# A routed adapter kernel: one chunk of the first weight is asked for behind two copies of x

## The reference

```python
def reference(x, itok_B_3_7, L0_cond_weight):
    # x (128, 32, 512) f32, itok_B_3_7 (128,) int32 from 3 to 7, L0_cond_weight (8, 512, 512) f32
    w = L0_cond_weight[itok_B_3_7]
    return x + jnp.einsum('bsi,boi->bso', x, w)
```

## Time and profile before

| | |
|---|---|
| median of three runs | 108.26 us (107.31 to 108.94) |
| the profiled execution, its own time | 106.55 us |
| its span in the trace | 104.8 us |
| TensorE busy | 98.7 us, 94% of the span |
| VectorE, ScalarE, GpSimd busy | 53.0, 56.0 and 42.4 us |
| granted clock of TensorE, mean | 0.994 |
| moved by DMA | 22.92 MB, 219 GB/s on average |

### The profile page before, as it was taken

How to read it: one execution, slowest core, us unless ns; L and a number is a source line. 1 busy time by engine, 2 the same in 40 slices (tenths; PEclk the granted TensorE clock), 3 DMA queues, 4 the chain that set the end, 5 groups by cost and what they waited for, 6 DMA issues and landing times.

```text
span 104.8 us, 2302 instructions
## 1 busy us (share of the span) xinstructions
PE 98.7 (94%) x447; PEld 80.3 (77%) x447; DVE 53.0 (51%) x107; ACT 56.0 (53%) x103; POOL 42.4 (40%) x58
## 2 busy tenths in 40 slices
PE   5969999999999999999999999999999999999960
PEld 3538888888888888888888888888888888888830
DVE  1289972595206964690378424862458247701000
ACT  5048333496424972883379443964388439633220
POOL 6757135007530466066304860276114731743000
PEclk9999999999999999999999999999999999999997
DMA  0994789849995799899963896457636783450633
GB/s 4 285 299 129 177 277 345 274 105 315 363 364 171 183 355 370 276 287 354 333 193 95 250 291 217 122 184 229 216 90 200 218 275 103 161 199 31 202 100 100
DMA packets 25089, 22.92 MB, mean 219 GB/s; under 512 B 3266, under 2 KB 20163, under 8 KB 25075
## 3 DMA queue, kind: packets, MB, share of 16 engines
q1 hardware_dynamic: 19442, 9.45, 32.4%
q0 software_dynamic: 2608, 8.06, 20.7%
q10 hardware_dynamic: 3024, 5.24, 15.9%
HBM read 17.30 MB, written 8.91 MB: 250 GB/s over the span
## 4 chain that ended last, share of the span: by engine, by line
PE 90%; DMA 3%; DVE 2%; issue 1%; ACT 1%; SPq 0%; DVEq 0%
PE out_ps L519 88%; DMA ids_i<-in_ids 3%; PE warm_ps L493 1%; ACT out_tile L342 1%; DVE in_slot L423 1%; SPq L197 0%; PE slot_ps L506 0%; DVE is_own L403 0%; DVE masked L420 0%; PE rank_ps L509 0%; DVE own_rank_b L428 0%; DVE masked L405 0%; DVE place_no L416 0%; DVE at_of L426 0%; PE out_ps L499 0%
## 5 line engine op out<-in xcount | busy, mean ns | idle before, releaser
L285 POOL DMA_INDIRECT out<-out_tile,row_of x31 | 35.1, 1132 | 50.5 <-ACT out_tile L342 40.5
L519 PE MATMUL out_ps<-w_hi,xt_hi 128*128 (+1 forms) x136 | 53.0, 390 | 0.0
L519 PE MATMUL out_ps<-w_lo,xt_hi 128*128 (+1 forms) x136 | 52.9, 389 | 0.0
L437 DVE TENSOR_TENSOR xt_lo<-x_raw,xt_hi 128x512 fp32r<-128x512 f32 x34 | 23.5, 691 | 32.6 <-ACT xt_hi L313 21.6
L519 PE MATMUL out_ps<-w_hi,xt_lo 128*128 (+1 forms) x136 | 36.5, 389 | 0.0
L313 ACT ACTIVATE xt_hi<-x_raw 128x512 fp32r<-128x512 f32 (+1 forms) x35 | 21.4, 615 | 26.8 <-DMA x_raw<-in_x 26.8
L519 PEld LDWEIGHTS out_ps<-w_hi,xt_hi 128*128 128x128 f32 x136 | 25.5, 188 | 5.4
L519 PEld LDWEIGHTS out_ps<-w_hi,xt_lo 128*128 128x128 f32 x136 | 25.5, 188 | 5.3
L519 PEld LDWEIGHTS out_ps<-w_lo,xt_hi 128*128 128x128 f32 x136 | 25.5, 188 | 5.3
L335 ACT ACTIVATE w_hi<-w_raw 128x512 fp32r<-128x512 f32 x32 | 18.4, 622 | 12.6 <-DVE w_raw L174 9.1
L342 ACT ACTIVATE out_tile<-out_ps 128x512 f32<-128x512 f32 x34 | 19.9, 586 | 5.5 <-PE out_ps L519 5.4
(11 more groups left out here) (58 smaller groups left out, 10.5 us busy)
## 6 DMA issues: line engine op xcount, KB each, us to landing
x_raw<-in_x SPq DMA_DIRECT2D x130, 64.0 KB
w_raw<-in_weight ACTq DMA_DIRECT2D x6, 1024.0 KB
w_raw<-in_weight ACTq DMA_DIRECT2D x6, 256.0 KB, 3.8
w_raw<-in_weight SPq DMA_DIRECT2D x2, 256.0 KB, 4.4
out<-out_tile,row_of POOLq DMA_INDIRECT x31
out<-out_tile ACTq DMA_DIRECT2D x6, 64.0 KB, 2.0
out<-out_tile SPq DMA_DIRECT2D x6, 64.0 KB, 1.9
x_raw<-in_x POOLq DMA_DIRECT2D x4, 64.0 KB, 2.3
```

The source lines that it names most:

```text
L285: nc.gpsimd.indirect_dma_start(out=out_rows, out_offset=bass.IndirectOffsetOnAxis(ap=row_of[:, t:t + 1], axis=0), in_=out_tile[n][:, :], i ...
L437: nc.vector.tensor_tensor(xt_lo[t % XT_BUFS][:, :, :, :], x_raw[t % X_BUFS][:, :, :, :].rearrange("p m c r -> p c m r"), xt_hi[t % XT_BUFS ...
L519: return nc.tensor.matmul(out_ps[n][:, :], lefts[left][k][:, c, :, :].rearrange("p m r -> p (m r)"), rights[right][:, bass.ds(rank, 1), c, ...
```

## The change

SyncE's request for chunk 3 of the first weight moves from before its wait for `first_found` to a place behind its two copies of x of tile 0 and ahead of the four of tile 1. The semaphore that it raises, the buffer and the size stay, and no wait is added.

```diff
@@ -196,7 +196,7 @@
         def _(sp):
             sp.dma_start(ids_row[:, :], ids.rearrange("(o b) -> o b", o=1)).then_inc(ids_row_loaded, 16)
             sp.dma_start(ids_i[:, :], ids.rearrange("(b o) -> b o", o=1)).then_inc(ids_loaded, 16)
-            load_rank_0(sp, (1, 3))
+            load_rank_0(sp, (1,))
...
@@ -213,6 +213,7 @@
             sp.wait_ge(first_found, 1)
             first = values_of(SP_ENGINE, first_at, slice(0, FIRST_TILES * SEQS), B)
             load_tile(0, first[0:2])
+            load_rank_0(sp, (3,))
             load_tile(1, first[SEQS:2 * SEQS])
```

## The result

The changed kernel takes **107.85 us** (median of 22 runs, 107.02 to 108.53), the kernel before 107.47 us beside it (22 runs, 106.55 to 108.94). The ratio is 1.0053, with a 95% interval of 1.0029 to 1.0078: half a per cent slower. This ratio leaves out the runs of a kernel that are over 1.5% slower than its fastest, which are five of the kernel before and none of the changed one; over all 22 and 22 the means differ by 0.30 us and the medians by 0.38. The fastest runs differ by 0.47 us (107.02 against 106.55). So the loss is 0.3 to 0.5 us. I had forecast 108.2, no change, from the sum of -0.08 us. The measured time lies in the range, but that is in part luck: the range stood about a median of three runs, 108.26, and 22 runs of the same kernel have 107.47. The direction was wrong: the change costs up to half a microsecond, where I had it gain less than 0.1.

A forecast was written before the change was run, and what follows sets the result against it. TensorE's unbroken products from 8.61 to 101.20 us were taken as the bound. A gain of 0.08 us at their start and costs of 0 gave 106.5 against the profiled 106.55, or 108.2 off the 108.26 median; range 107.0 to 109.0.

The forecast's parts named there:

- x of tile 0 comes sooner: Opening: x lands at about 6.95 us, 0.9 sooner, but the warm-ups last to 8.33; gain 0.08 us.
- The other parent: Start of TensorE's products: besides routing, they wait for tile 0's first half of xt_hi, holding TensorE by 0.08 us.
- Chunk 3 comes later: First weight's chunk 3 lands at 7.95 us, in time for tile 0's last product; cost 0, 0.30 us at T = 9.45.
- The limit of 9.15: Latest landing of chunk 3, in us, before TensorE stops at tile 0's last product, which stands at 11.04.
- ScalarE's order: ScalarE's sequence of roundings: earlier x pulls w_hi 2 forward, w_hi 3 starts at 8.48 us; cost 0.
- GpSimd is held: GpSimd's requests for x of tile 3 move by 1.0 us; x comes at 13.85, at worst 15.3, limit 16.0; cost 0.
- SyncE's queue: SyncE's copies for tile 1 move by one issue, 0.43 us, and tile 2 by 0.1 at most; cost 0.
- C: Rival: TensorE waits for chunk 3 at tile 0's last three products, hole 0.3 to 1.3 us, 108.5 to 109.5; chance 0.10.
- A: Rival: x of tile 0 gates the timed runs, so the change gives back up to 0.9 us, 107.4; chance 0.16.
- B: Rival: routing in the opening starts sooner too, ids_i landing up to 0.8 us sooner, 107.5; chance 0.06.
- D: Rival: the queue order does nothing and x of tile 0 still lands at 7.85 us, time 108.26; chance 0.10.
- The clock sentence of C: TensorE's opening: nothing added for the clock, granted 1.00 though busy only 0.39 us from 6 to 7; no row shows a fall.

The follow-up runs named there:

- r8: The kernel before, with GpSimd's addition to chunk 1 held until slots_ready; one execution, no ratio given, in_slot took 0.30 us.
- r3: The kernel before, with GpSimd held until w_hi of chunk 2 is rounded before it asks for x of tile 3; ratio to before 1.0134.
- r6: The kernel before, with VectorE instead of GpSimd adding the identity to chunk 3; ratio to before 0.9982.
- r12: The kernel before, with four instead of eight warm-up matmuls right ahead of tile 0; ratio to before 1.0002.
- r2: The changed kernel, with VectorE instead of GpSimd adding the identity to chunk 3; ratio to before 0.9959.
- r4: The changed kernel, with ScalarE's requests for all four chunks of weight 1 behind its rounding of x of tile 3; ratio to before 1.0096.
- r10: The kernel of r2, with VectorE's addition to chunk 3 behind its w_lo of chunk 2 instead of ahead; ratio to before 1.0053.
- r11: The kernel of r2, with four instead of eight warm-up matmuls right ahead of tile 0; ratio to before 0.9969.
- r1: The changed kernel unaltered, run again beside the kernel before; ratio to before 1.0045.
- r5: The changed kernel, with SyncE asking for x of tile 3 behind tile 2 in place of GpSimd; ratio to before 1.0171.
- r7: The kernel of r2 run again unaltered; ratio to before 0.9954.
- r9: The kernel of r2, with GpSimd held until xt_lo of tile 0 before it asks for x of tile 3; ratio to before 1.0122.

## Why the prediction was wrong

1. *x of tile 0 comes sooner*: right, about 1.0 us (6.85 against 7.88, 0.9 forecast). The gain, 0.08 forecast, is 0.25 in the trace. The step took the routing chain as a fixed parent of the start. It ended 0.18 us sooner (warm-ups from 7.38 instead of 7.56), because in_slot met no addition's start there, which is chance (r8). The other parent was under-priced: the trace of before has x of tile 0 the earliest of the five traces with chunk 3 asked for early (7.88; 7.97 to 8.14 in r3, r6, r8 and r12). Where TensorE was quick enough to be held by x, it started at 8.44, 8.64 and 8.69 (before, r6, r12), against 8.16 to 8.33 in the quick traces with chunk 3 late (the change, r2, r4, r10, r11).

2. *Chunk 3 comes later*: its landing was mis-sized. I took 7.95, by the shortest copy of all (3.2 us), and it took 4.0 in the change, 4.1 in r1, r5 and r7 and 4.3 in r4, landing at 8.7 to 9.2. The limit of 9.15 was also too late: it counted from a start that the change moved by 0.25, and with an addition that takes 0.45 us by itself but 0.52, 0.91 and 0.86 when VectorE is busy with its subtractions (change, r1, r4). My upper bound of the cost, 0.30 us, was passed in r4 (0.70).

3. *ScalarE's order*: right, nothing late by it. (7.88 + 0.72 + 0.6 is 9.2, not 9.1; nothing hangs on it.)

4. *GpSimd is held*: **the step that failed.** It saw the mechanism, priced it with four copies of 2.3 us wherever they stand, and gave 15.3 at worst against a limit of 16.0. The requests began at 10.09 instead of 9.5, in a trace where chunk 3 was 0.8 later than I took it, and the last copy took 4.56 us since it now stood beside weight 1's chunks, whose requests at 11.42 to 13.0 were in the trace of before. So of the 3.65 us by which x of tile 3 came later (16.48 against 12.83), 1.62 is the later request, which the step had as 1.0, and 2.0 is the longer copy, which it had at nothing. The limit was too late too: the change's chain has 0.24 us from the end of the rounding to the product, which the step left out, and tile 3's turn came at 16.54 with the earlier start, so x was needed by 15.66 (16.54 - 0.64 - 0.24), not 16.0. r3 and r9 show the cost of late requests alone, r4 shows that the neighbours are weight 1's chunks. The claim that what stands behind is caught up held for ScalarE, but not for TensorE.

5. *SyncE's queue*: right here (x of tile 2 met at 11.99 instead of 11.81, in time); r5 shows that four requests more on it are too many.

Of the rivals, C (chunk 3 as TensorE's wait) had 0.10 and is a part of the truth: r10 has it at 0.55 us. The other half had no rival of its own; it stood under "costed at nothing". A is borne out only in kind: x of tile 0 came up to 0.26 us later in other traces than in the one of before, not 0.9. The excess of the timed runs lies for the most part elsewhere, in TensorE's slow pace in the opening, which hides the change's loss. B is not borne out either: is_own started at 4.17, not before 4.1. D fell with 6.85.

The clock sentence of C was right for its trace: no row of before showed a fall behind its 0.39 us of work from 6 to 7. r3's trace shows a fall to 0.50 behind 0.18 us in the same stretch, and r11's shows none behind 0.21. The slow pace of r1 and r7 comes and goes between executions of kernels with the same instructions (the first trace of the change, and r2). The rule of the Trainium skill on ring order ("DMA: Bandwidth & Descriptors", "Queues, rings and completion order") agrees with the traces on both sides of the change: x of tile 0 left the queue ahead of chunk 3 and landed a microsecond sooner. The same section says that an engine alternates between the rings that have work; r4 fits this: GpSimd's copies took 2.5 us at most when ScalarE's ring had no weight in it.

## What to carry to other kernels

When a request moves, follow the engine that waits for it in program order and price what it asks for next at the place where that now falls: here copies of the same 64 KB took 2.2 to 5.8 us to land, by what was in flight beside them. Take the time of the moved copy from the copies it will share with, not from the shortest. And if an early operand is worth buying, free the engine that serves the late one first: the change alone lost 0.3 to 0.5%; with VectorE's addition the loss was gone, and the pair was 0.4% ahead of the kernel before in both comparisons, clear of the noise in one.

## What the runs showed of the hardware

- 64 KB copies asked for by GpSimd took 2.1 to 2.6 us with SyncE's stream beside them, where the last was asked for by 10.5 us (before, r2, r6, r7, r8, r10, r11, r12), and 2.3 to 2.5 where weight 1 was held back (r4), and up to 4.0, 4.6, 5.6 and 5.8 us where the last was asked for at 11.9 to 12.7, about when three 256 KB copies of ScalarE were (r1, the change, r9, r3).
- An addition of 128x128 on GpSimd took 0.45 us alone and 0.81 to 0.91 us beside VectorE's 128x512 subtractions (r1, r4, r5), but 0.52 in the change. The subtraction that started while the addition ran took 0.94 or 0.95 us instead of 0.68 (r1, r5, the change); in r4, where the subtraction started first, it kept its 0.68. The rows of r1, GpSimd and VectorE:

```profile
8.96 0.91 POOL L174 TENSOR_TENSOR w_raw<-w_raw,identity 128x128 f32<-128x128 f32 x1 [2.20 <-DMA w_raw<-in_weight]
...
9.47 0.94 DVE L433 TENSOR_TENSOR w_lo<-w_raw,w_hi 128x512 fp32r<-128x512 f32 x1
```

- A 128x156 operation on VectorE (in_slot) took 0.52 to 0.58 us where such an addition started within 0.03 us of it, and 0.30 or 0.31 otherwise, also in the middle of one. In the change, where in_slot started 0.09 us ahead of an addition, in_slot kept its 0.30 and the addition took 0.52:

```profile
6.17 0.52 POOL L174 TENSOR_TENSOR w_raw<-w_raw,identity 128x128 f32<-128x128 f32 x1
```

- Eight warm-up matmuls took 1.05 us in six traces (before, the change, r2, r4, r6, r10), 1.24 in r9 and 1.76 to 1.89 in r1, r5, r7 and r8, with a granted clock that reads 1.00 in all of them; in r3 they took 1.89 as the clock fell. The start of the products moves with it, by 1.35 us between r2 and r7, the same kernel, whose executions differ by 1.37 us (106.25 and 107.62).
